# Attention issued in another order over four pairs at once, with the scores on four banks and two banks shared by the rest

## The chip, the cores and the metric

One core of a Trainium2 chip runs the whole program. The metric is the device time of one execution in microseconds (us). The engines are TensorE (PE; its weight loads are listed apart as PEld), VectorE (DVE), ScalarE (ACT), GpSimd (POOL) and SyncE (SP), each with an instruction queue of its own that runs in order and is tied to the others by semaphores only.

## The reference, cut to what matters

The program is four layers one behind the other on `x` of shape (8, 512, 128): attention with relative positions, a mixture of 8 experts, a layer trained at test time, a mixture of 16 experts, each followed by `_layernorm(x + layer(x))`. The change touches the first layer alone:

```python
B, S, D = hidden_states.shape                       # 8, 512, 128; N_HEADS 16, D_KV 64
q = (hidden_states @ Wq).reshape(B, S, N_HEADS, D_KV)      # k and v alike
bias = compute_bias(rel_bias_table, S, S)
scores = jnp.einsum('bqhd,bkhd->bhqk', q, k) * (1.0 / math.sqrt(D_KV)) + bias
attn = jax.nn.softmax(scores, axis=-1)
ctx = jnp.einsum('bhqk,bkhd->bqhd', attn, v).reshape(B, S, N_HEADS * D_KV)
return ctx @ Wo
```

## The kernel before, in words

`kernel` runs `prepare`, `attention`, `ffn_0`, `ttt_layer` and `ffn_1` as phases with a barrier between them. `attention` (L201) works on pairs of heads: 16 heads are 8 pairs, and 8 batches make 64 pairs, one step each, with two more steps to drain. Numbers that need more than fp32r are kept as a high and a low half: ScalarE copies a PSUM bank to fp32r (the high half), VectorE subtracts that from the bank (the low half), and only then is the bank free. A product of two such numbers is three matmuls (`PASSES`).

For one pair the work is:
- TensorE projects q (L386) and k (L387) with `project`, three matmuls of 512 columns each, and one block of values (`make_values`, L308: two token tiles, four heads, six matmuls of 256 columns).
- `scores` (L316), four times, one for each tile of 128 queries: three passes, each for both heads, on the upper and the lower 64 rows, into the two banks `score_ps`. VectorE adds the bias, negates and takes the row's smallest (`score`, L505, and the DVE_READ_ACCUMULATOR behind it); ScalarE takes the exponential and its sum (`exps`, L443).
- `turn` (L326), eight times, four for each head: four transposes of probabilities into one of two banks `turn_ps`, copied by ScalarE (L431) and completed by VectorE (`rest_of_turn`, L515). Turn g waits for the low half of turn g-2.
- `context` (L336), twice: eight matmuls of values with turned probabilities into `ctx_ps`; ScalarE copies it (`copy_context`, L437).
- `add_head` (L349), twice: four fp32 products (eight matmul records) with `wo` into `out_ps`; VectorE scales by the inverse sums (`scale_head`, L523), POOL adds to `x` (`add`, L272).

The order of the work is written out by hand, once for each engine, in `step` (TensorE L358, ScalarE L448, VectorE L532, POOL L280). In step s the scores of pair s stand between the turns, context 0 and output 0 of pair s-1 and output 1 of pair s-2; q and k of pair s+1 are projected in its middle. The values of pairs 0 to 5 are made in their own step, those of pairs 6 and 7 both in step 6 of a batch (`value_pairs`, L263). In step 7, POOL having staged a copy of the next batch's rows (`stage`, L269), TensorE turns x (`turn_rows`, L297) into the only `xT`.

The eight PSUM banks are two for scores, two for turns, two (`misc_ps`) for q, k, values and x, one for contexts, one for outputs. A block of scores therefore waits until VectorE has read the block before (L320).

Of the kernel before, what the change touches and what calls it, by code (L numbers as in the profile page):

```python
# [17 lines left out]
P = 128  # L18
# [182 lines left out]
def attention(core, ins, keep):  # L201
# [4 lines left out]

    nc = core.nc
# [7 lines left out]
    GW = GROUP * D_KV  # L215
    with ExitStack() as st:
        two = lambda name, shape, dt=F32: [core.sb(st, f"{name}{i}", shape, dt) for i in range(2)]

        rows = core.sb(st, "rows", [P, QT, D])
        xT = two("xT", [P, SEQ], F32R)  # L220
        q, k = ([two(f"{n}_{i}", [P, SEQ], F32R) for i in range(2)] for n in "qk")
# [4 lines left out]
        negmax, total = two("negmax", [P, QT, 2]), two("total", [P, QT, 2])  # L226
        inv = [core.sb(st, f"inv{i}", [P, QT, 2]) for i in range(4)]
# [6 lines left out]
        names = ("score_done", "scored", "exp_done", "inv_ready", "turn_done", "turned_hi", "turned_lo", "ctx_done", "ctx_ready",  # L234
                 "val_done", "val_hi", "val_lo", "qk_done", "qk_hi", "qk_lo", "staged", "x_turned", "x_hi", "x_lo", "sum_done", "scaled_ready", "added")
        (score_done, scored, exp_done, inv_ready, turn_done, turned_hi, turned_lo, ctx_done, ctx_ready,
         val_done, val_hi, val_lo, qk_done, qk_hi, qk_lo, staged, x_turned, x_hi, x_lo, sum_done, scaled_ready, added) = (core.sem(n) for n in names)
        block = st.enter_context(nc.Block())

        def steps_of(step):  # L240

            for s in range(STEPS + 2):
                step(s, s // PAIRS, s % PAIRS, s >= STEPS - PAIRS)

        bias_in, wo_in = [core.sem(f"bias_in{i}") for i in range(HEADS // 2)], core.sem("wo_in")
# [11 lines left out]
        is_step = lambda s: 0 <= s < STEPS  # L257
        after = lambda s, n: s >= n
        head = lambda a: slice(a * D_KV, (a + 1) * D_KV)
        tile_of = lambda i: slice(i * P, (i + 1) * P)  # L260
        wide = lambda w, r: w[:, r * P:(r + 1) * P]

        def value_pairs(r):  # L263

            return ((r, 0),) if r < 6 else ((6, 0), (7, 1)) if r == 6 else ()

        @block.gpsimd
        def _(pool):
            def stage(b):  # L269
                pool.tensor_copy(rows[:, :, :], x[:, b * QT:(b + 1) * QT, :]).then_inc(staged, 1)  # L270

            def add(back, b, r, a):  # L272

                pool.wait_ge(scaled_ready, 2 * back + a + 1)
                if after(back, 1) or a:
                    pool.wait_ge(added, 2 * back + a)
                mine = x[:, b * QT:(b + 1) * QT, :]
                pool.tensor_tensor(mine, mine, scaled[a][:, :, :], ALU.add).then_inc(added, 1)  # L278

            def step(s, b, r, last):  # L280
                back, earlier = s - 1, s - 2
                if after(s, 2) and is_step(earlier):
                    add(earlier, b if r >= 2 else b - 1, (r - 2) % PAIRS, 1)
                if after(s, 1) and is_step(back):
                    add(back, b if r >= 1 else b - 1, (r - 1) % PAIRS, 0)
                if r == 3 and not last and is_step(s):
                    pool.wait_ge(x_turned, b + 1)
                    stage(b + 1)

            pool.wait_ge(x_in, 16)  # L290
            stage(0)
            steps_of(step)
            pool.wait_ge(added, HEADS * BATCH)

        @block.tensor
        def _(pe):
            def turn_rows(b):  # L297
                pe.wait_ge(staged, b + 1)
                for j in range(QT):
                    mm = pe.transpose(misc_ps[0][:, tile_of(j)], rows[:, j, :], ident[:, :])  # L300
                mm.then_inc(x_turned, 1)

            def project(to, w, r):
                for n, (u, v) in enumerate(PASSES):
                    mm = pe.matmul(to[:, :], wide(w[u], r), xT[v][:, :], start=(n == 0), stop=(n == 2))
                mm.then_inc(qk_done, 1)

            def make_values(b, n, m):  # L308
                group, first = n // 2, n % 2 * 2
                for t in range(2):  # L310
                    for i, (u, v) in enumerate(PASSES):
                        mm = pe.matmul(misc_ps[m][:, t * GW:(t + 1) * GW], xT[u][:, tile_of(first + t)], wv[v][:, group * GW:(group + 1) * GW],
                                       start=(i == 0), stop=(i == 2))
                mm.then_inc(val_done, 1)

            def scores(s, p, i):  # L316
                if i == 0:
                    pe.wait_ge(qk_lo, 2 * s + 2)
                if after(s, 1) or i >= 1:
                    pe.wait_ge(scored, 8 * s + 2 * i)  # L320
                for n, (u, v) in enumerate(PASSES):
                    for a in range(2):
                        mm = pe.matmul(score_ps[a][:, :], q[p][u][head(a), tile_of(i)], k[p][v][head(a), :], start=(n == 0), stop=(n == 2))  # L323
                mm.then_inc(score_done, 1)

            def turn(back, p, g):  # L326
                a, c = g // QT, g % QT
                if c == 0:
                    pe.wait_ge(exp_done, 8 * back + 7 + a)
                if after(back, 1) or g >= 2:  # L330
                    pe.wait_ge(turned_lo, 8 * back + g - 1)
                for t in range(QT):
                    mm = pe.transpose(turn_ps[g % 2][:, tile_of(t)], prob[p][a][:, t, tile_of(c)], ident[:, :])  # L333
                mm.then_inc(turn_done, 1)

            def context(back, r, a):  # L336

                if after(back, 1) or a:
                    pe.wait_ge(ctx_ready, 2 * back + a)
                if a == 0 and r % 2 == 0:  # L340
                    pe.wait_ge(val_lo, (back - r) + r + 2)
                for c in range(QT):
                    pe.wait_ge(turned_lo, 8 * back + QT * a + c + 1)
                    for n in range(2):
                        mm = pe.matmul(ctx_ps[:, :], val[r // 2 % 2][:, c, r % 2 * 2 + a, :], probT[n][:, c, :],  # L345
                                       start=(c == 0 and n == 0), stop=(c == QT - 1 and n == 1))
                mm.then_inc(ctx_done, 1)

            def add_head(back, b, r, a):  # L349

                pe.wait_ge(ctx_ready, 2 * back + a + 1)
                if after(back, 1) or a:
                    pe.wait_ge(scaled_ready, 2 * back + a)
                for t in range(QT):
                    mm = pe.matmul(out_ps[:, tile_of(t)], ctxT[a][:, tile_of(t)], wo[:, 2 * r + a, :], start=True, stop=True)  # L355
                mm.then_inc(sum_done, 1)

            def step(s, b, r, last):  # L358
                p, back, earlier = r % 2, s - 1, s - 2
                now, turns, sums = is_step(s), after(s, 1) and is_step(back), after(s, 2) and is_step(earlier)  # L360
                br = (r - 1) % PAIRS
                if now:
                    scores(s, p, 0)
                if turns:
                    turn(back, 1 - p, 0)
                    turn(back, 1 - p, 1)
                if now:
                    for n, m in value_pairs(r):
                        make_values(b, n, m)
                    if r == PAIRS - 1 and not last:  # L370
                        turn_rows(b + 1)
                if sums:
                    add_head(earlier, b if r >= 2 else b - 1, (r - 2) % PAIRS, 1)
                if now:
                    scores(s, p, 1)
                if turns:
                    turn(back, 1 - p, 2)
                    turn(back, 1 - p, 3)
                if now and not (last and r == PAIRS - 1):
                    if r == PAIRS - 1:  # L380
                        pe.wait_ge(x_lo, b + 2)
                    elif r == PAIRS - 2:
                        pe.wait_ge(val_lo, PAIRS * b + PAIRS)
                    else:
                        pe.wait_ge(val_lo, PAIRS * b + r + 1)
                    project(misc_ps[1], wq, (r + 1) % PAIRS)  # L386
                    project(misc_ps[0], wk, (r + 1) % PAIRS)  # L387
                if now:
                    scores(s, p, 2)
# [2147 lines left out]
```

## Time and profile before

| | before |
|---|---|
| median of 3 runs | 2408.22 us (2405.91 to 2409.17) |
| the profiled execution | 2398.8 us, span 2397.1 us |
| TensorE busy | 1935.5 us, 81% |
| VectorE busy | 1660.8 us, 69% |
| ScalarE busy | 1198.1 us, 50% |
| POOL busy | 587.8 us, 25% |

The span is the time from the first to the last instruction. Busy time is the union of an engine's instructions. Durations of matmuls overlap, because they are pipelined, so what a matmul holds of the engine is read from the distance to the next start.

### The profile page before, as it was taken

Reading aid. Unit: us, or ns where it says so; the run is one execution under the profiler, and the core shown is the slowest. Engines: PE = TensorE matmul, PEld = TensorE weight load, DVE = VectorE, ACT = ScalarE, POOL = GpSimd, SP = SyncE. Lnnn points to the kernel's source line nnn. Section 1 sums busy time; section 2 is a strip of 40 time slices with the busy share of each in tenths; the row PEclk is TensorE's granted clock in tenths of the full one; section 3 lists DMA queues with packets and bytes.
Section 4 is the critical chain, followed back from the end, with each engine's and each line's share of the span. In section 5 each row is a group of like instructions: output and inputs, shape, how many; then the busy total and the mean of one; then the engine's idle time right before and its main releaser. Section 6 shows DMA issues by size and latency. Waiting matters only on the chain. (4 is left out here: it accounts for less than half of the span.)

```text
span 2397.1 us, 35530 instructions
## 1 busy us (share of the span) xinstructions
PE 1935.5 (81%) x11500; PEld 1484.7 (62%) x11500; DVE 1660.8 (69%) x4000; ACT 1198.1 (50%) x2714; POOL 587.8 (25%) x629
## 2 busy tenths in 40 slices
PE   6999999999999999994789142999989998932771
PEld 4777777777777777773667132777767776711761
DVE  5888888888888888875465677677567755557433
ACT  5777777777777777772033232233223322240432
POOL 0111111111111111110345615443133411000372
PEclk9999999999999999995699566999999999965896
DMA  6000000000000000003044100000000000022243
GB/s 205 1 1 1 1 1 1 1 1 1 1 1 1 1 1 1 1 1 99 27 111 115 49 20 0 1 0 0 1 1 0 0 0 3 1 65 71 74 96 84
DMA packets 60472, 62.37 MB, mean 26 GB/s; under 512 B 6560, under 2 KB 50032, under 8 KB 60064
## 3 DMA queue, kind: packets, MB, share of 16 engines
q1 hardware_dynamic: 49936, 43.79, 5.9%
q0 software_dynamic: 10384, 16.66, 3.5%
q8 instruction: 82, 1.34, 0.2%
q14 instruction: 70, 0.57, 0.1%
HBM read 41.36 MB, written 18.81 MB: 25 GB/s over the span
## 5 line engine op out<-in xcount | busy, mean ns | idle before, releaser
L517 DVE TENSOR_TENSOR probT<-turn_ps,probT 128x512 fp32r<-128x512 f32 x512 | 346.5, 687 | 81.3 <-ACT probT L435 72.1
L445 ACT ACTIVATE prob<-prob,negmax 128x512 f32<-128x512 f32 x512 | 371.2, 725 | 60.8 <-DVE negmax L512 56.9
L278 POOL TENSOR_TENSOR x<-x,scaled 128x512 f32<-128x512 f32 x128 | 165.1, 1290 | 897.2 <-DVE scaled L529 897.2
L435 ACT CAST probT<-turn_ps 128x512 fp32r<-128x512 f32 x512 | 297.2, 581 | 127.7 <-PE turn_ps L333 127.7
L512 DVE CUSTOM_DVE_ANT_0 prob<-score_ps,bias 128x512 f32<-128x512 f32 x512 | 332.4, 686 | 1.4 <-issue 1.4
L333 PE MATMUL turn_ps<-ident,prob 128*128 128x128 f32 x2048 | 290.4, 279 | 39.1 <-DVE probT L517 34.5
L333 PEld LDWEIGHTS turn_ps<-ident,prob 128*128 128x128 f32 x2048 | 223.0, 140 | 137.4 <-DVE probT L517 101.8
L345 PE MATMUL ctx_ps<-probT,val 128*128 128x512 f32 x1024 | 270.1, 405 | 0.0
L323 PE MATMUL score_ps<-k,q 64*128 64x512 f32 x1536 | 247.5, 427 | 5.7 <-DVE negmax L512 4.3
L345 PEld LDWEIGHTS ctx_ps<-probT,val 128*128 128x128 f32 x1024 | 177.8, 188 | 61.8 <-issue 23.0
L323 PEld LDWEIGHTS score_ps<-k,q 64*128 64x128 f32 x1536 | 124.6, 185 | 82.4 <-issue 35.0
L1358 POOL TENSOR_TENSOR w<-c,vc 128x512 f32<-128x512 f32 x64 | 82.9, 1295 | 218.2 <-DVE c L1470 218.2
L355 PE MATMUL out_ps<-wo,ctxT 128*128 128x128 f32 x1024 | 135.4, 275 | 0.7 <-ACT ctxT L441 0.7
L1430 ACT CAST dpT_hi<-pred_ps 128x128 fp32r<-128x128 f32 x64 | 17.1, 267 | 232.6 <-PE pred_ps L1377 232.6
L355 PEld LDWEIGHTS out_ps<-wo,ctxT 128*128 128x128 f32 x1024 | 124.8, 192 | 1.2 <-ACT ctxT L441 1.1
L441 ACT COPY ctxT<-ctx_ps 128x512 f32<-128x512 f32 x128 | 75.7, 592 | 54.8 <-PE ctx_ps L345 54.8
L445 ACT ACTIVATION_READ_ACCUMULATOR prob<-prob,negmax 128x1 f32 x512 | 96.9, 189 | 0.0
L529 DVE TENSOR_TENSOR scaled<-out_ps,inv 128x512 f32<-128x512 f32 x128 | 87.4, 683 | 2.7 <-PE out_ps L355 2.7
L1463 DVE TENSOR_TENSOR s<-u_ps,sg 128x512 f32<-128x512 f32 x64 | 44.3, 692 | 55.6 <-ACT sg L1435 55.6
L939 ACT COPY xgT<-x_ps 128x128 f32<-128x128 f32 x80 | 21.3, 266 | 109.0 <-PE x_ps L887 96.7
L1398 PEld LDWEIGHTS dwp_ps<-dp,h 128*128 128x128 f32 x512 | 67.0, 191 | 5.9
L150 PE MATMUL tt<-ident,x 128*128 128x128 f32 x32 | 6.5, 396 | 79.0 <-PEq L1778 79.0
(489 smaller groups left out, 4095.5 us busy)
## 6 DMA issues: line engine op xcount, KB each, us to landing
ew<-L_ffn_fc_weight SPq DMA_DIRECT2D x32, 256.0 KB
bias<-bias_line SPq DMA_DIRECT2D x16, 448.0 KB, 9.5
mid_rows<-row SPq DMA_DIRECT2D x40, 128.0 KB
last_rows<-row SPq DMA_DIRECT2D x40, 64.0 KB
rows_dram<-rows SPq DMA_DIRECT2D x1, 2304.0 KB, 18.6
acc_dram<-zero POOLq DMA_DIRECT2D x1, 2112.0 KB, 16.9
acc<-acc_dram SPq DMA_DIRECT2D x4, 528.0 KB
x_rows<-x SPq DMA_DIRECT2D x4, 512.0 KB, 6.1
```

Source lines behind the costliest of these rows:

```text
L278: pool.tensor_tensor(mine, mine, scaled[a][:, :, :], ALU.add).then_inc(added, 1)
L323: mm = pe.matmul(score_ps[a][:, :], q[p][u][head(a), tile_of(i)], k[p][v][head(a), :], start=(n == 0), stop=(n == 2))
L333: mm = pe.transpose(turn_ps[g % 2][:, tile_of(t)], prob[p][a][:, t, tile_of(c)], ident[:, :])
L345: mm = pe.matmul(ctx_ps[:, :], val[r // 2 % 2][:, c, r % 2 * 2 + a, :], probT[n][:, c, :], start=(c == 0 and n == 0), stop=(c == QT - 1 an ...
L355: mm = pe.matmul(out_ps[:, tile_of(t)], ctxT[a][:, tile_of(t)], wo[:, 2 * r + a, :], start=True, stop=True)
L435: act.copy(probT[0][:, g % QT, :], turn_ps[g % 2][:, :]).then_inc(turned_hi, 1)
L441: act.copy(ctxT[a][:, :], ctx_ps[:, :]).then_inc(ctx_ready, 1)
L445: act.activation(prob[p][a][:, i, :], prob[p][a][:, i, :], ACT.Exp, bias=negmax[p][:, i, a:a + 1], scale=-1.0, accum_out=total[p][:, i, a: ...
L512: dve.tensor_tensor_reduce(prob[p][a][:, i, :], score_ps[a][:, :], bias[:, h, first:first + SEQ][:, ::-1], -1.0, 3.0e38, ALU.add, ALU.min, ...
L517: dve.tensor_tensor(probT[1][:, g % QT, :], turn_ps[g % 2][:, :], probT[0][:, g % QT, :].bitcast(F32), ALU.subtract).then_inc(turned_lo, 1)
L529: dve.tensor_tensor(scaled[a][:, :, :], out_ps[:, :].rearrange("p (t d) -> p t d", t=QT), inv[r % 4][:, :, a:a + 1].to_broadcast([P, QT, D ...
L1358: pool.tensor_tensor(w[r][:, :], c1[p][:, :], vc[p][:, :], ALU.mult).then_inc(w_ready, 1)
```

## The change

Four pairs are in work at once in `attention`; the arithmetic and the number of instructions stay, but for POOL's copy of the rows and the second wait on exponentials. Scores get four banks, two blocks of two; `work[0]` holds queries, values and context 0, `work[1]` keys, context 1, both outputs and the turned rows. `xT` and the sums get more buffers, x is turned in pair 5 of a batch straight from `x`, and the exponentials count on one semaphore per head. Each engine has one flat list per step. `is_pair(p)` is `0 <= p < 64`, `turns_x(s)` is true in pair 5 of all batches but the last; copies and subtractions are those of before on the new banks.

```diff
-        xT = two("xT", [P, SEQ], F32R)
...
+        xT, q, k = ([two(f"{n}_{i}", [P, SEQ], F32R) for i in range(2)] for n in ("xT", "q", "k"))
...
-        score_ps, turn_ps = [bank("score_ps0"), bank("score_ps1")], [bank("turn_ps0"), bank("turn_ps1")]
-        misc_ps = [bank("misc_ps0"), bank("misc_ps1")]
-        ctx_ps, out_ps = bank("ctx_ps"), bank("out_ps")
...
+        score_ps = [[bank(f"score_ps{i}_{a}") for a in range(2)] for i in range(2)]
+        turn_ps, work = [bank("turn_ps0"), bank("turn_ps1")], [bank("work_ps0"), bank("work_ps1")]
...
         @block.tensor
...
+            def turn_next_rows(s):
+                if turns_x(s):
+                    pe.wait_ge(scaled_ready, 2 * (s - 2) + 2)
+                    turn_rows(batch_of(s) + 1)
...
+            def queries(p):
...
+                    if p % PAIRS == 0:
+                        pe.wait_ge(x_lo, batch_of(p) + 1)
+                    if p >= 1:
+                        pe.wait_ge(val_lo, p)
+                    project(work[0], wq, p)
+            def keys(p):
...
+                    if turns_x(p - 1):
+                        pe.wait_ge(x_lo, batch_of(p) + 2)
+                    elif p >= 3:
+                        pe.wait_ge(scaled_ready, 2 * (p - 3) + 2)
+                    elif p >= 1:
+                        pe.wait_ge(qk_lo, 2 * p)
+                    project(work[1], wk, p)
+            def values(p):
...
+                    if p >= 2:
+                        pe.wait_ge(ctx_ready, 2 * (p - 2) + 1)
...
+            def scores(p, i):
...
+                    if i == 0:
+                        pe.wait_ge(qk_lo, 2 * p + 2)
+                    if p >= 1 or i >= 2:
+                        pe.wait_ge(scored, 8 * p + 2 * i - 2)
+                    for n, (u, v) in enumerate(PASSES):
+                        for a in range(2):
+                            mm = pe.matmul(score_ps[i % 2][a][:, :], q[p % 2][u][head(a), tile_of(i)], k[p % 2][v][head(a), :],
+                                           start=(n == 0), stop=(n == 2))
...
+            def context(p, a):
...
+                    if a == 1:
+                        pe.wait_ge(scaled_ready, 2 * p + 1)
+                    elif p + 2 < STEPS:
+                        pe.wait_ge(qk_lo, 2 * (p + 2) + 1)
...
+            def add_head(p, a):
...
+                    pe.wait_ge(ctx_ready, 2 * p + a + 1)
+                    if a == 0:
+                        if p + 2 < STEPS:
+                            pe.wait_ge(qk_lo, 2 * (p + 2) + 2)
...
+            def step(s):
+                turn(s - 1, 1)
+                add_head(s - 2, 1)
+                queries(s + 1)
+                turn(s - 1, 2)
+                turn(s - 1, 3)
+                turn_next_rows(s)
+                scores(s, 2)
+                scores(s, 3)
+                keys(s + 1)
+                context(s - 1, 0)
+                turn(s - 1, 4)
+                turn(s - 1, 5)
+                scores(s + 1, 0)
+                scores(s + 1, 1)
+                add_head(s - 1, 0)
+                turn(s - 1, 6)
+                turn(s - 1, 7)
+                values(s + 1)
+                context(s - 1, 1)
+                turn(s, 0)
...
         @block.scalar
...
+            def step(s):
+                exps(s, 0, 0)
+                copy_values(s)
+                exps(s - 1, 3, 1)
+                copy_context(s - 2, 1)
+                turn(s - 1, 0)
+                turn(s - 1, 1)
+                exps(s, 0, 1)
+                exps(s, 1, 0)
+                copy_qk(s + 1, 0)
+                copy_next_rows(s)
+                turn(s - 1, 2)
+                turn(s - 1, 3)
+                exps(s, 1, 1)
+                copy_qk(s + 1, 1)
+                copy_context(s - 1, 0)
+                turn(s - 1, 4)
+                exps(s, 2, 0)
+                turn(s - 1, 5)
+                exps(s, 2, 1)
+                exps(s, 3, 0)
+                turn(s - 1, 6)
+                turn(s - 1, 7)
...
         @block.vector
...
+            def step(s):
+                score(s, 0, 1)
+                rest_of_values(s)
+                invert(s - 1)
+                score(s, 1, 0)
+                rest_of_turn(s - 1, 0)
+                rest_of_turn(s - 1, 1)
+                scale_head(s - 2, 1)
+                score(s, 1, 1)
+                rest_of_qk(s + 1, 0)
+                rest_of_next_rows(s)
+                score(s, 2, 0)
+                rest_of_turn(s - 1, 2)
+                rest_of_turn(s - 1, 3)
+                rest_of_qk(s + 1, 1)
+                score(s, 2, 1)
+                score(s, 3, 0)
+                score(s, 3, 1)
+                rest_of_turn(s - 1, 4)
+                rest_of_turn(s - 1, 5)
+                score(s + 1, 0, 0)
+                scale_head(s - 1, 0)
+                rest_of_turn(s - 1, 6)
+                rest_of_turn(s - 1, 7)
```

## Rows read from the trace of the kernel before

**Rows 1.** Stretch, us; busy PE, PEld, DVE, ACT, POOL; PEclk, DMA share, GB/s.

```profile
16.00:1082.60 1066.60, 1014.48 (x6432) 757.79 (x6432) 864.35 (x2184) 815.16 (x1864) 169.37 (x136) 1.00 0.03 9
412.00:543.40 131.40, 126.42 (x805) 94.58 (x804) 107.99 (x273) 101.86 (x233) 21.21 (x18) 1.00 0.00 1
1082.60:2397.10 1314.50, 917.39 (x5064) 726.50 (x5064) 792.99 (x1813) 377.76 (x844) 417.53 (x487) 0.83 0.14 37
```

**Rows 2.** Waits, one batch (412.0 to 543.4 us): total, times, longest.

```profile
PE turn_ps L333 <- DVE probT L517: 4.3, 8, 0.5
```

**Rows 3.** Timeline of TensorE through one pair: start, us, operation.

```profile
444.77 0.98 PE L323 MATMUL score_ps<-k,q 64*128 64x512 f32 x6
445.68 1.09 PE L333 MATMUL turn_ps<-ident,prob 128*128 128x128 f32 x8
446.53 0.36 PE L312 MATMUL misc_ps<-wv_hi,xT 128*128 128x256 f32 x1
...
447.33 1.05 PE L355 MATMUL out_ps<-wo,ctxT 128*128 128x128 f32 x8
448.31 0.97 PE L323 MATMUL score_ps<-k,q 64*128 64x512 f32 x6
449.22 1.09 PE L333 MATMUL turn_ps<-ident,prob 128*128 128x128 f32 x8
450.16 0.73 PE L305 MATMUL misc_ps<-xT,wq_hi 128*128 128x512 f32 x2
450.73 0.39 PE L305 MATMUL misc_ps<-xT,wq_lo 128*128 128x512 f32 x1
450.96 0.62 PE L305 MATMUL misc_ps<-xT,wk_hi 128*128 128x512 f32 x2
451.43 0.40 PE L305 MATMUL misc_ps<-xT,wk_lo 128*128 128x512 f32 x1
451.75 0.97 PE L323 MATMUL score_ps<-k,q 64*128 64x512 f32 x6
452.65 2.13 PE L345 MATMUL ctx_ps<-probT,val 128*128 128x512 f32 x8
454.63 1.03 PE L333 MATMUL turn_ps<-ident,prob 128*128 128x128 f32 x8
455.59 0.96 PE L323 MATMUL score_ps<-k,q 64*128 64x512 f32 x6
456.63 0.66 PE L333 MATMUL turn_ps<-ident,prob 128*128 128x128 f32 x4
457.82 0.66 PE L333 MATMUL turn_ps<-ident,prob 128*128 128x128 f32 x4 [0.53 <-DVE probT L517]
458.31 1.06 PE L355 MATMUL out_ps<-wo,ctxT 128*128 128x128 f32 x8
459.12 2.09 PE L345 MATMUL ctx_ps<-probT,val 128*128 128x512 f32 x8
461.14 0.96 PE L323 MATMUL score_ps<-k,q 64*128 64x512 f32 x6
```

**Rows 4.** Timeline of ScalarE in the same pair.

```profile
455.26 0.59 ACT L435 CAST probT<-turn_ps 128x512 fp32r<-128x512 f32 x1 [0.55 <-PE turn_ps L333]
455.75 0.73 ACT L445 ACTIVATE prob<-prob,negmax 128x512 f32<-128x512 f32 x1
...
456.46 0.57 ACT L435 CAST probT<-turn_ps 128x512 fp32r<-128x512 f32 x1
```

**Rows 5.** Timeline of VectorE in the same pair.

```profile
445.94 0.69 DVE L512 CUSTOM_DVE_ANT_0 prob<-score_ps,bias 128x512 f32<-128x512 f32 x1
...
446.55 0.69 DVE L512 CUSTOM_DVE_ANT_0 prob<-score_ps,bias 128x512 f32<-128x512 f32 x1
...
455.88 0.69 DVE L517 TENSOR_TENSOR probT<-turn_ps,probT 128x512 fp32r<-128x512 f32 x1 [0.20 <-ACT probT L435]
```

**Rows 6.** Timeline of POOL at the start of attention.

```profile
15.79 0.61 POOL L270 COPY rows<-x 128x512 f32<-128x512 f32 x1 [14.26 <-POOLq L79]
```

More of the change, by code:

```diff
@@ L225, in attention @@
         ctxT = two("ctxT", [P, SEQ])
-        negmax, total = two("negmax", [P, QT, 2]), two("total", [P, QT, 2])
-        inv = [core.sb(st, f"inv{i}", [P, QT, 2]) for i in range(4)]
+        negmax = two("negmax", [P, QT, 2])
+        total, inv = ([core.sb(st, f"{n}{i}", [P, QT, 2]) for i in range(4)] for n in ("total", "inv"))
         scaled = two("scaled", [P, QT, D])
@@ L255, in _ @@
                     sp.dma_start(wo[half, :, :], ins["L0_attn_Wo"].rearrange("(h p) d -> p h d", p=D_KV)).then_inc(wo_in, 16)
[L257 to L265, printed above, removed]
         @block.gpsimd
         def _(pool):
[L269 to L288, printed above, removed]
-            pool.wait_ge(x_in, 16)
-            stage(0)
-            steps_of(step)
+            pool.wait_ge(x_in, 16)
+            for p in range(STEPS):
+                mine = x[:, batch_of(p) * QT:(batch_of(p) + 1) * QT, :]
+                for a in range(2):
+                    pool.wait_ge(scaled_ready, 2 * p + a + 1)
+                    if p or a:
+                        pool.wait_ge(added, 2 * p + a)
+                    pool.tensor_tensor(mine, mine, scaled[a][:, :, :], ALU.add).then_inc(added, 1)
             pool.wait_ge(added, HEADS * BATCH)
@@ L304, in project @@
+            def project(to, w, p):
                 for n, (u, v) in enumerate(PASSES):
-                    mm = pe.matmul(to[:, :], wide(w[u], r), xT[v][:, :], start=(n == 0), stop=(n == 2))
+                    mm = pe.matmul(to[:, :], wide(w[u], p), xT[batch_of(p) % 2][v][:, :], start=(n == 0), stop=(n == 2))
                 mm.then_inc(qk_done, 1)
[L308 to L383, printed above, removed]
-                    else:
[L385 to L389, printed above, removed]
-                if turns:
-                    context(back, br, 0)
-                    turn(back, 1 - p, 4)
-                    turn(back, 1 - p, 5)
-                if now:
-                    scores(s, p, 3)
-                if turns:
-                    turn(back, 1 - p, 6)
-                    turn(back, 1 - p, 7)
-                    if s == 1:
-                        pe.wait_ge(wo_in, 32)
-                    add_head(back, b if r >= 1 else b - 1, br, 0)
-                    context(back, br, 1)
@@ new lines, in values @@
+            def values(p):
+                if is_pair(p):
+                    if p >= 2:
+                        pe.wait_ge(ctx_ready, 2 * (p - 2) + 1)
+                    else:
+                        pe.wait_ge(qk_lo, 2 * p + 1)
+                    group, first, xs = p % PAIRS // 2, p % 2 * 2, xT[batch_of(p) % 2]
+                    for t in range(2):
+                        for i, (u, v) in enumerate(PASSES):
+                            mm = pe.matmul(work[0][:, t * GW:(t + 1) * GW], xs[u][:, tile_of(first + t)], wv[v][:, group * GW:(group + 1) * GW],
+                                           start=(i == 0), stop=(i == 2))
+                    mm.then_inc(val_done, 1)
@@ new lines, in turn @@
+            def turn(p, g):
+                if is_pair(p):
+                    a, c = g // QT, g % QT
+                    if c == 0:
+                        pe.wait_ge(exp_done[a], QT * (p + 1))
+                    if p >= 1 or g >= 2:
+                        pe.wait_ge(turned_lo, 8 * p + g - 1)
+                    for t in range(QT):
+                        mm = pe.transpose(turn_ps[g % 2][:, tile_of(t)], prob[p % 2][a][:, t, tile_of(c)], ident[:, :])
+                    mm.then_inc(turn_done, 1)
@@ new lines, in context @@
+            def context(p, a):
+                if is_pair(p):
+                    if a == 1:
+                        pe.wait_ge(scaled_ready, 2 * p + 1)
+                    elif p + 2 < STEPS:
+                        pe.wait_ge(qk_lo, 2 * (p + 2) + 1)
+                    else:
+                        pe.wait_ge(ctx_ready, 2 * (p - 1) + 1)
+                    if a == 0 and p % 2 == 0:
+                        pe.wait_ge(val_lo, p + 2)
+                    for c in range(QT):
+                        pe.wait_ge(turned_lo, 8 * p + QT * a + c + 1)
+                        for n in range(2):
+                            mm = pe.matmul(work[a][:, :], val[p // 2 % 2][:, c, p % 2 * 2 + a, :], probT[n][:, c, :],
+                                           start=(c == 0 and n == 0), stop=(c == QT - 1 and n == 1))
+                    mm.then_inc(ctx_done, 1)
@@ new lines, in add_head @@
+            def add_head(p, a):
+                if is_pair(p):
+                    pe.wait_ge(ctx_ready, 2 * p + a + 1)
+                    if a == 0:
+                        if p + 2 < STEPS:
+                            pe.wait_ge(qk_lo, 2 * (p + 2) + 2)
+                        else:
+                            pe.wait_ge(scaled_ready, 2 * p)
+                    if p == 0 and a == 0:
+                        pe.wait_ge(wo_in, 32)
+                    for t in range(QT):
+                        mm = pe.matmul(work[1][:, tile_of(t)], ctxT[a][:, tile_of(t)], wo[:, 2 * (p % PAIRS) + a, :], start=True, stop=True)
+                    mm.then_inc(sum_done, 1)
@@ new lines, in copy_values, with turn @@
+            def copy_values(p):
+                if is_pair(p):
+                    act.wait_ge(val_done, p + 1)
+                    if p >= 4 and p % 2 == 0:
+                        act.wait_ge(ctx_done, 2 * (p - 3) + 2)
+                    first = p % 2 * 2
+                    act.copy(val[p // 2 % 2][:, first:first + 2, :, 0:D_KV],
+                             work[0][:, :].rearrange("p (t h d) -> p t h d", t=2, h=GROUP)).then_inc(val_hi, 1)
+            def turn(p, g):
+                if is_pair(p):
+                    act.wait_ge(turn_done, 8 * p + g + 1)
+                    if g % QT == 0 and (g or p >= 1):
+                        act.wait_ge(ctx_done, 2 * p + g // QT)
+                    act.copy(probT[0][:, g % QT, :], turn_ps[g % 2][:, :]).then_inc(turned_hi, 1)
@@ L482, in _ @@
             copy_rows(0)
-            copy_qk(0, 0, 0)
-            copy_qk(0, 0, 1)
-            steps_of(step)
+            for s in range(-1, STEPS + 2):
+                step(s)
         @block.vector
@@ L570, in _ @@
             rest_of_rows(0)
-            rest_of_qk(0, 0, 0)
-            rest_of_qk(0, 0, 1)
-            steps_of(step)
+            for s in range(-1, STEPS + 2):
+                step(s)
 class Norms:
```

239 lines of the change are left out of this document (91 added, 148 removed).

## The prediction

> **What bounds the kernel now.** I read the busy time of each engine by stretch first. Attention is the stretch from 16.0 to 1082.6 us, 1066.6 of the 2397.1 us span, and the only one that the diff touches. TensorE is busy for 1014.5 us of it, VectorE for 864.4, ScalarE for 815.2, all at a granted clock of 1.00 (the 2.4 GHz level) [rows 1]. One batch of eight pairs takes 131.4 us, 16.42 us a pair; a plain pair takes 461.14 - 444.77 = 16.37 us [rows 1, 3]. In a pair VectorE is busy 108.0/8 = 13.5 us and ScalarE 101.9/8 = 12.7 us, so TensorE sets the pace: its matmuls lie idle for only 4.3 us per batch, all of it before the turning of probabilities, waiting for VectorE's low half of an earlier turn [rows 2].
>
> Then the timeline of TensorE through one pair, read by the distance from one start to the next, since the durations overlap [rows 3]. What a reader is to see there:
> - A full 512-column matmul holds the engine 0.23 us (450.73 to 450.96). Six projections are 1.39, a context of eight is 1.86, and 1.98 where it follows scores (452.65 to 454.63).
> - A turn of four transposes is 0.44 (eight from 449.22 to 450.16 take 0.94, restart included); an output of eight small matmuls 0.89 (447.33 to 448.31 is 0.98 with the passage to scores); the six 256-column matmuls of the values 0.71 (446.53 to 447.33 with their first load).
> - A block of scores has six matmuls that run two at a time on the upper and lower 64 rows, so three slots, 3 x 0.23 = 0.69. It really takes 0.91 from its first start to the next block's (444.77 to 445.68; 0.90 at 451.75). Ahead of it the preceding block is 0.10 too long (451.43 would be followed at +0.23; the four slots from 450.16 to 451.75 are 1.59 for 1.39, of which about 0.10 is the restart of the first), and the work behind it starts 0.05 to 0.12 slow. So each block alone costs about 0.38 beyond its slots, 1.5 us a pair for four.
> - Two stalls: 455.59 to 456.63 is 1.04 for a block that takes 0.91 (0.13), and 456.63 to 457.82 is 1.19 for a turn of 0.44 (0.70 with its slow restart of 0.05 taken off).
>
> The ledger of a pair: eight turns 3.49, two contexts 3.72, two outputs 1.79, projections 1.39, values 0.71, scores 4 x (0.69 + 0.38) = 4.28: 15.38 us of work. The rest of 16.37, 0.99, is the 0.83 of stalls, two restarts of 0.05 behind them, and 0.05 that I can't place.
>
> **The change, part by part.**
> (1) Scores on four banks in blocks of two. Each pair now issues scores 2 and 3 together, and 0 and 1 of the next pair together. Block 1 no longer waits until VectorE has emptied block 0, so the engine passes into and out of the 64-row form twice a pair and not four times: 2 x 0.38 saved, less the restarts that stay, 0.75 a pair. No row of before has two blocks side by side, so the bounds are: nothing saved, if the six-slot run is broken at its middle, and 0.75. Inside a block the second and third slot follow at 0.23 [rows 3], and the second block has the same shapes and the same rows of the array; I take 0.75.
> For the reason behind the 0.38 the Trainium skill ("TensorEngine Tiling (Array Packing)", Key Properties) has a rule: changing the tiling mode, not just the tile, drains the engine. The trace agrees with a loss at the edges (0.10 ahead of a block, 0.22 in its 0.91 beyond three slots [rows 3]); that it is absent between blocks of the same mode no run here shows yet. By that rule the sum is the one I take; if each block paid it whatever its neighbour, the time would be that of rival B.
>
> (2) The order. Whether the stalls go, I find by walking one pair of the new order with the lengths above. Zero is the start of turn 1 of pair s-1. TensorE without waits: turn 1 at 0; output (s-2, 1) 0.44; queries 1.33; turns 2 and 3 2.02; scores 2 at 3.00, scores 3 at 3.79; keys 4.57; context 0 5.37; turns 4 and 5 7.23; scores 0 and 1 of s+1 at 8.20 and 8.99; output (s-1, 0) 9.77; turns 6 and 7 10.72; values 11.59; context 1 12.33; turn 0 of pair s 14.19; end 14.62. That is the ledger again with half the passages: 3.49 + 3.72 + 1.79 + 1.39 + 0.71 + 3.5 = 14.6.
> The handovers: from the first transpose of a turn to ScalarE's copy 0.63 (454.63 to 455.26), from there to VectorE 0.62 (455.26 to 455.88), from there back to TensorE 0.75 (455.88 to 456.63); from a block of scores to VectorE 1.17 (444.77 to 445.94). On ScalarE a copy holds 0.49, an exponential with its read 0.71; on VectorE an operation holds 0.61 [rows 3 to 5].
> ScalarE then comes out as: context copy (s-2, 1) at -0.23, turn copies 0.25 and 0.72, two exponentials to 2.63, the query copy, turn copies 3.10 and 3.57, an exponential, the key copy not before 5.57 (it waits for the keys, and the context copy and all turns are queued behind it), context copy 7.43, turn copies 7.90 and 9.10, 11.40 and 11.87, values 13.06. VectorE: low halves of turns 0 and 1 at 0.86 and 1.46, scaling 2.07, score (1, 1) 2.67, queries 3.28, score (2, 0) 4.15, turns 2 and 3 4.77 and 5.38, keys 6.17, scores 6.78, 7.40, 8.01, turns 4 and 5 8.62 and 9.70, score and scaling 10.31 and 10.99, turns 6 and 7 12.0 and 12.6, values 13.82, the reciprocals behind the last exponential 14.46, score (1, 0) 14.58.
> Against TensorE's needs: turn 2 needs the low half of turn 0 at 1.61, 0.4 early; scores 3 wait for score (1, 1), 0.3 early; keys for the scaling (2.82), 1.7 early; context 0's fourth chunk for turn 3 (6.13), 0.6 early; scores (s+1, 1) for score (3, 1) at 8.79, 0.2 early; turn 7 for turn 5's low half (10.45), 0.7 early; context 1 for turn 7's (13.35), 1.0 early; output (s-2, 1) needs the context copy at 0.42 and stands at 0.44: no slack at all. So the 0.99 goes, and what is late next is that output, with 0 to 0.2 us a pair. VectorE's 13.5 and ScalarE's 12.7 busy us still fit into 14.62. I take 0.05 for it.
>
> (3) Two shared banks. Queries, values and context 0 pass through one, keys, both outputs, context 1 and x through the other. The waits that this adds are in the walk (keys behind scaling, values behind the context copy of 8.1, context 1 behind the scaling of 11.7) and none is last.
>
> (4) x. Its four transposes stay (0.44 a batch) but move to pair 5, into the second buffer. They wait for the scaling of 2.82 and start at 2.90; the keys behind them start at 5.01 and need x's low half at about 4.93. Gain and loss both under 0.1 a batch. POOL's copy of x's rows goes; it is hidden in seven batches and costs its 0.61 once, at 15.79, where nothing else runs [rows 6]. The additions to x on POOL are the same two per pair, 21.2 us busy in 131.4.
>
> (5) Total buffers, semaphores for exponentials, the order of SP's loads: the same instructions, nothing queued behind them; 0, with ±1 us for both ends of attention. The first pair's lone steps and the last pair's drain keep their chains, only about the last 3 us of each could shift.
>
> The sum: 16.37 - 0.75 - 0.99 + 0.05 = 14.68 a pair. A batch is 8 x 14.68 + 0.44 for x: 117.9 against 131.4, 13.5 a batch, 108 us for eight, and 0.6 at the start. The profiled execution has 2398.8 us around a span of 2397.1 and goes to 2290; the median of the runs shown is 2408.2, 0.4% above it, and goes to 2299. The rest, 1314.5 us at a mean clock of 0.83 [rows 1], is the same program and starts 109 us earlier; that its clock falls and rises at other moments I allow 5 us.
>
> **The rivals.**
> A. New small stalls. In-order ScalarE waits 0.8 us for the keys and 1.4 for context 0 with turns queued behind; if handovers are some tenths slower than my rows, 0.3 to 0.8 us a pair comes back: 64 x 0.3 to 0.8, 2318 to 2350. For it: output (s-2, 1) has no slack, scores only 0.2. Against: most have 0.4 and more.
> B. The double blocks save nothing: +0.75 x 64 = 48, 2347. For it: no row shows such a run, and a wait stands at its middle. Against: waits that are already met cost nothing in the rows of turns and outputs (458.31, 459.12).
> C. The other side: a shared bank is handed over late. A full loop from the writer over ScalarE and VectorE back to the writer is 2.0 us (454.63 to 456.63 [rows 3 to 5]). A pair has seven such handovers on two banks. If one lies bare per pair, it costs 2.0 and eats the whole gain of 1.69: 16.68 a pair, 64 x 0.31 = 20 slower, 2428. It decides from 1.69 us of bare handover a pair. Against: the smallest distance on either bank is 0.1 (x in one pair of eight), else over 1 us.
> D. The change doesn't do what it says: VectorE's queue becomes the pace at its 13.5 busy us plus waits for ScalarE of about 2 (it waits 8 times in my walk): 15.5 a pair, 0.8 x 64 = 51 more, 2350.
>
> **How the numbers follow.** Forecast (2288 to 2312) 0.58; A 0.2; B 0.08; D 0.07; C 0.05; the rest, no change, 0.02. Two executions of one kernel differ by up to 0.14% here, so a difference under 0.2% (5 us) can't be told from none. Faster holds the forecast, A, B and D: 0.93; same 0.02; slower 0.05. The range for 8 in 10 goes from 2285 (no stall at all, clock luck) to 2340, most of A.
>
> **What would show it.** Starts of turn 0 of successive pairs 14.6 to 14.8 us apart; TensorE's idle before turns gone from 4.3 us a batch to under 0.5; the second of two score blocks 0.23 behind the last slot of the first, and six slots from first start to next block in about 1.6; ScalarE waiting once a pair for context 0 and once for the keys; the clock still 1.00. Wrong would be a pair of over 15.2 us, waits at keys, values or context 1 for a scaling (C), or 0.33 and not 0.23 at the middle of a double block (B).

## The result, and the profile after

| | before | changed |
|---|---|---|
| median | 2407.5 us (4 runs) | 2299.4 us (2297.1 to 2300.7, 4 runs) |
| ratio to before | | 0.9555, 95% interval 0.9543 to 0.9568 |
| profiled execution | 2398.8 us, span 2397.1 | 2297.1 us, span 2295.4 |
| attention's last addition ends | 1082.6 us | 980.9 us |
| one pair of heads | 16.37 us | 14.7 us |

The changed kernel is 4.5% faster. Busy times by stretch come first, with the columns of [rows 1]: attention, one batch, and all that follows.

```profile
16.00:980.90 964.90, 953.93 (x6432) 786.27 (x6431) 860.25 (x2184) 797.77 (x1864) 166.57 (x128) 1.00 0.03 10
400.00:517.90 117.90, 117.90 (x805) 97.79 (x804) 107.21 (x274) 99.61 (x233) 20.79 (x16) 1.00 0.00 1
980.90:2295.40 1314.50, 919.43 (x5064) 725.45 (x5064) 793.47 (x1813) 376.74 (x844) 417.72 (x488) 0.83 0.14 37
```

Against [rows 1]: TensorE is busy in all of the 117.9 us, and the clock is 1.00 as before. The two stretches called a batch were cut at 131.4 and 117.9 us; counted from a pair's first scores to those of the eighth pair behind it, and past the first two pairs, a batch takes 131.3 to 131.5 us before and 117.9 to 118.2 after (117.6 at the end, where no x is turned). Behind attention stand the same 1314.5 us at the same mean clock of 0.83. So in the profiled executions all of the 101.7 us lie in attention.

The waits of that batch (total, times, longest). TensorE's matmuls waited for 4.3 us in [rows 2] and have no row any more. The longest waits left, POOL's aside, are those of ScalarE and VectorE, the engines that do not set the pace:

```profile
ACT ctxT L442 <- PE work_ps L358: 10.0, 8, 1.3
DVE probT L521 <- ACT probT L435: 7.3, 23, 0.4
ACT k L419 <- PE work_ps L286: 5.5, 8, 0.8
...
ACT probT L435 <- PE turn_ps L341: 2.5, 8, 0.3
```

TensorE's timeline through one pair, to be read by the distance from start to start as [rows 3]:

```profile
407.15 1.03 PE L341 MATMUL turn_ps<-ident,prob 128*128 128x128 f32 x8
408.02 1.12 PE L373 MATMUL work_ps<-wo,ctxT 128*128 128x128 f32 x8
408.90 0.70 PE L286 MATMUL work_ps<-xT,wq_hi 128*128 128x512 f32 x2
...
409.67 1.03 PE L341 MATMUL turn_ps<-ident,prob 128*128 128x128 f32 x8
410.64 1.66 PE L329 MATMUL score_ps<-k,q 64*128 64x512 f32 x12
412.23 0.73 PE L286 MATMUL work_ps<-xT,wk_hi 128*128 128x512 f32 x2
...
413.03 1.99 PE L358 MATMUL work_ps<-probT,val 128*128 128x512 f32 x8
414.86 1.03 PE L341 MATMUL turn_ps<-ident,prob 128*128 128x128 f32 x8
415.82 1.69 PE L329 MATMUL score_ps<-k,q 64*128 64x512 f32 x12
417.44 1.16 PE L373 MATMUL work_ps<-wo,ctxT 128*128 128x128 f32 x8
418.44 1.04 PE L341 MATMUL turn_ps<-ident,prob 128*128 128x128 f32 x8
419.23 0.36 PE L317 MATMUL work_ps<-wv_hi,xT 128*128 128x256 f32 x1
...
420.02 2.01 PE L358 MATMUL work_ps<-probT,val 128*128 128x512 f32 x8
421.87 1.04 PE L341 MATMUL turn_ps<-ident,prob 128*128 128x128 f32 x8
422.75 1.12 PE L373 MATMUL work_ps<-wo,ctxT 128*128 128x128 f32 x8
```

From 407.15 to 421.87 is 14.72 us. Zero of the prediction's walk is turn 1, half of the first row and of the last but one (two turns each, so 0.44 behind their starts, at 407.59). The walk put the output at 0.44, the queries at 1.33, turn 2 at 2.02, scores 2 at 3.00; the rows have 0.43, 1.31, 2.08 and 3.05. Twelve score matmuls, 410.64 to 412.23, take 1.59 where two blocks of [rows 3] took 0.91 each; from the last slot of the first block to the first of the second are 0.23, as between any two slots. Keys stand at 4.64 (walk 4.57), context 0 at 5.44 (5.37), scores 0 at 8.23 (8.20), output 0 at 9.85 (9.77), turns 6 and 7 at 10.85 (10.72, the largest miss), values at 11.64 (11.59).

ScalarE's copy of context (s-2, 1) in the next pair, the place that the walk gave no slack:

```profile
422.07 0.59 ACT L442 COPY ctxT<-work_ps 128x512 f32<-128x512 f32 x1
```

It ends at 422.66, and the output that needs it starts at 422.75.

### The profile page after: what moved, and what is told of

Same layout as the page of the kernel before. It is cut to its first block and busy times, and to the rows that moved or that the text cites. A ratio compares the mean times of both kernels' runs of the same rounds, so it can differ in the third digit from the quotient of the medians.

```text
span 2295.4 us, 35504 instructions
## 1 busy us (share of the span) xinstructions
PE 1877.2 (82%) x11500; PEld 1512.4 (66%) x11500; DVE 1657.2 (72%) x4000; ACT 1179.7 (51%) x2714; POOL 585.0 (25%) x621
## 5 line engine op out<-in xcount | busy, mean ns | idle before, releaser
L341 PE MATMUL turn_ps<-ident,prob 128*128 128x128 f32 x2048 | 266.3, 273 | 1.3 <-DVE probT L521 1.1
L358 PE MATMUL work_ps<-probT,val 128*128 128x512 f32 x1024 | 257.2, 393 | 0.1
L341 PEld LDWEIGHTS turn_ps<-ident,prob 128*128 128x128 f32 x2048 | 236.7, 140 | 28.2 <-DVE probT L521 3.4
L329 PE MATMUL score_ps<-k,q 64*128 64x512 f32 x1536 | 215.4, 412 | 3.5 <-DVE negmax L515 2.1
L358 PEld LDWEIGHTS work_ps<-probT,val 128*128 128x128 f32 x1024 | 187.4, 188 | 39.9 <-DVE probT L521 1.7
L373 PE MATMUL work_ps<-wo,ctxT 128*128 128x128 f32 x1024 | 146.0, 286 | 0.7 <-ACT ctxT L442 0.7
L373 PEld LDWEIGHTS work_ps<-wo,ctxT 128*128 128x128 f32 x1024 | 123.9, 191 | 26.1 <-issue 22.4
L1423 ACT CAST dpT_hi<-pred_ps 128x128 fp32r<-128x128 f32 x64 | 17.1, 266 | 234.4 <-PE pred_ps L1370 234.4
L442 ACT COPY ctxT<-work_ps 128x512 f32<-128x512 f32 x128 | 75.1, 587 | 84.5 <-PE work_ps L358 83.5
L536 DVE TENSOR_TENSOR scaled<-work_ps,inv 128x512 f32<-128x512 f32 x128 | 87.9, 686 | 2.7 <-PE work_ps L373 2.7
L1399 PE MATMUL pred_ps<-proj,hT 128*128 128x128 f32 x512 | 68.7, 278 | 1.4 <-ACT hT L1437 1.4
```

The source lines that it names most:

```text
L329: mm = pe.matmul(score_ps[i % 2][a][:, :], q[p % 2][u][head(a), tile_of(i)], k[p % 2][v][head(a), :], start=(n == 0), stop=(n == 2))
L341: mm = pe.transpose(turn_ps[g % 2][:, tile_of(t)], prob[p % 2][a][:, t, tile_of(c)], ident[:, :])
L358: mm = pe.matmul(work[a][:, :], val[p // 2 % 2][:, c, p % 2 * 2 + a, :], probT[n][:, c, :], start=(c == 0 and n == 0), stop=(c == QT - 1 a ...
L373: mm = pe.matmul(work[1][:, tile_of(t)], ctxT[a][:, tile_of(t)], wo[:, 2 * (p % PAIRS) + a, :], start=True, stop=True)
L442: act.copy(ctxT[a][:, :], work[a][:, :]).then_inc(ctx_ready, 1)
L536: dve.tensor_tensor(scaled[a][:, :, :], work[1][:, :].rearrange("p (t d) -> p t d", t=QT), inv[p % 4][:, :, a:a + 1].to_broadcast([P, QT, ...
```

## The experiments

**Double blocks taken apart**, both, and one of the two:

```diff
                 scores(s, 2)
-                scores(s, 3)
                 keys(s + 1)
+                scores(s, 3)
...
                 scores(s + 1, 0)
-                scores(s + 1, 1)
                 add_head(s - 1, 0)
+                scores(s + 1, 1)
```

> The changed kernel with both double blocks of scores taken apart: the keys stand between blocks 2 and 3, output 0 between blocks 0 and 1; banks and all other orders as in the change. Theory (a passage into and out of the 64-row form costs about 0.38 us each time, and the double blocks save two of the four): +0.75 us a pair, 64 x 0.75 = 48 us more than the changed kernel's 2299, so 2347; TensorE idle for nothing. Rival (only the new order counts, the passages cost nothing or are hidden): 2299 to 2303.

> Only blocks 2 and 3 taken apart by the keys, blocks 0 and 1 stay together. Theory: one passage more, 0.40 us a pair (exit 0.10, restart of a 512-column matmul 0.11, entry 0.10, slow first slot 0.10), 26 us, so 2325. Rival: nothing, 2299.

Measured: 2350.2 us with both apart (ratio to before 0.978, 0.976 to 0.980), 2330.1 in one run with blocks 2 and 3 apart. The pair is 15.51 and 15.13 us against 14.69: 0.82 for two passages more, 0.44 for one. TensorE's timeline with both apart:

```profile
399.31 1.04 PE L341 MATMUL turn_ps<-ident,prob 128*128 128x128 f32 x8
400.28 0.99 PE L329 MATMUL score_ps<-k,q 64*128 64x512 f32 x6
401.20 0.73 PE L286 MATMUL work_ps<-xT,wk_hi 128*128 128x512 f32 x2
401.77 0.39 PE L286 MATMUL work_ps<-xT,wk_lo 128*128 128x512 f32 x1
402.09 0.96 PE L329 MATMUL score_ps<-k,q 64*128 64x512 f32 x6
402.99 2.11 PE L358 MATMUL work_ps<-probT,val 128*128 128x512 f32 x8
```

Scores 2 are followed after 0.92, the keys' restart (0.57 for two matmuls, 0.34 + 0.23), entry into scores 3 0.32 behind the last key matmul (401.77), scores 3 again 0.90: the pattern of [rows 3] is back. The theory holds and the rival falls. The passages cost slightly more than I had (0.41 to 0.44 and not 0.38 each). In the pair of a batch that turns x the keys, one block earlier here, also wait 0.5 us for the low half of x; plain pairs have no wait of TensorE.

**The shared bank freed late**:

```diff
                 rest_of_turn(s - 1, 1)
-                scale_head(s - 2, 1)
+                if turns_x(s) or not is_pair(s):
+                    scale_head(s - 2, 1)
                 score(s, 1, 1)
...
                 rest_of_turn(s - 1, 3)
+                if is_pair(s) and not turns_x(s):
+                    scale_head(s - 2, 1)
                 rest_of_qk(s + 1, 1)
```

> The changed kernel with VectorE's scaling of output (s-2, 1) moved behind the low halves of turns 2 and 3, except in the pairs that turn x. It frees the shared bank for the keys at 6.74 us of the pair where the keys stand at 4.57. Theory (rival C of the prediction as a mechanism: one bare handover of a shared bank costs TensorE its whole length): 2.17 us a pair in about 55 pairs, 119 us, so 2418, slower than before the change. Rival (the queues have slack enough to take most of it up by shifting): under 1 us a pair, below 2354.

Measured: 2437.8 us, slower than before (1.0128, 1.0109 to 1.0147), as the theory said in its direction, and 20 us beyond its number. The mean pair of most batches is 17.1 us; but for the one that turns x (15.15, its scaling stands where it was) the pairs are of two kinds, 16.7 and 18.25. TensorE's timeline in one of 18.25, and four windows (columns of [rows 1]):

```profile
432.71 1.66 PE L329 MATMUL score_ps<-k,q 64*128 64x512 f32 x12
436.27 1.10 PE L286 MATMUL work_ps<-xT,wk_hi 128*128 128x512 f32 x2 [1.91 <-DVE scaled L536]
437.17 0.63 PE L286 MATMUL work_ps<-xT,wk_lo 128*128 128x512 f32 x1
437.60 3.04 PE L358 MATMUL work_ps<-probT,val 128*128 128x512 f32 x8
440.48 1.04 PE L341 MATMUL turn_ps<-ident,prob 128*128 128x128 f32 x8
```

```profile
423.19:559.81 136.62, 123.29 (x806) 101.28 (x805) 108.37 (x274) 99.62 (x234) 20.71 (x16) 0.96 0.00 1
436.70:439.70 3.00, 3.00 (x8) 2.30 (x7) 1.24 (x4) 0.59 (x1) 0.87 (x1) 0.50 0.00 0
437.60:440.50 2.90, 2.90 (x10) 2.24 (x9) 2.04 (x7) 0.59 (x1) 0.00 (x0) 0.61 0.00 0
444.10:461.10 17.00, 15.10 (x105) 12.52 (x104) 13.79 (x37) 12.63 (x31) 2.57 (x2) 1.00 0.00 0
```

The keys start at 436.27; they were due 1.6 behind the scores, at 434.30. That is the bare handover, 1.97 us. In the pair of 16.7 nothing else happens (window from 444.1, clock 1.00). In the pair of 18.25 the keys take 1.33 us (436.27 to 437.60) where they take 0.80 in the changed kernel, and the context behind them 2.88 (to 440.48) where it takes 1.83: 1.58 together. The granted clock says why: it is 0.50, the lower level of 1.2 GHz, from 436.7 to 439.7, and 0.61 over the whole context. The stall of 1.9 us once a pair had gone before, and TensorE was busy otherwise. So a bare handover costs its length and, in 21 of the 54 pairs that have it (mostly three of a batch), 1.6 us more through the clock: 54 x 1.97 + 21 x 1.6 = 140 us, and attention's last addition ends 139.3 us later than in the changed kernel (1120.2 against 980.9). Why one pair falls and the next, with the same stall, does not, no run shows.

The Trainium skill describes such a thing ("TensorE: Matmul & The Clock Gate", A second HAM failure mode: psum-queue depth-cycling): where a kernel cycles through PSUM banks, short idles between groups of matmuls make the clock swing between its two levels, and throughput is lost to the throttling and warming up. This run's trace agrees in the swing, with 0.96 over the batch; the next experiment, with a shorter stall, does not show it.

**The copy without slack, one place later**:

```diff
-                copy_context(s - 2, 1)
                 turn(s - 1, 0)
+                copy_context(s - 2, 1)
                 turn(s - 1, 1)
```

> The changed kernel with ScalarE's copy of context (s-2, 1) one place later, behind the copy of turn 0. Theory (output (s-2, 1) has no slack, so any delay of that copy goes straight into the pair): the copy starts 0.72 instead of -0.23 us, the output 0.93 late, 62 x 0.93 = 58 us, 2357, and no change of the clock, since the stall is under 1 us. Rival (the clock falls here as it does with longer stalls): 2375 or more. Second rival (slack in the queues takes it up): under 2315.

Measured: 2357.1 us in one run; the pair 15.6 us, 0.93 more. TensorE's timeline, turns 0 and 1 and the output behind them:

```profile
401.09 1.03 PE L341 MATMUL turn_ps<-ident,prob 128*128 128x128 f32 x8
402.85 1.16 PE L373 MATMUL work_ps<-wo,ctxT 128*128 128x128 f32 x8 [0.72 <-ACT ctxT L442]
...
416.71 1.04 PE L341 MATMUL turn_ps<-ident,prob 128*128 128x128 f32 x8
418.48 1.16 PE L373 MATMUL work_ps<-wo,ctxT 128*128 128x128 f32 x8 [0.73 <-ACT ctxT L442]
```

From the turns' start to the output are 1.76 us; in the changed kernel they were 0.88 (421.87 to 422.75). The whole delay comes through, and the clock stays at 1.00 in attention, so both rivals fall.

**VectorE loaded with one more operation** (result unused):

```diff
                 scale_head(s - 2, 1)
+                if is_pair(s):
+                    dve.tensor_tensor(spare[1][:, :], bias[:, 0, 0:SEQ], bias[:, 1, 0:SEQ], ALU.add)
                 score(s, 1, 1)
```

> The changed kernel with one more 128x512 sum of two SBUF tensors on VectorE in each pair, ahead of score (1, 1); its result is not used. Theory (VectorE has about 1.6 us of waits in a pair, and the place has 0.33 us of slack towards scores 3): of its 0.61 us only 0.28 shows, 64 x 0.28 = 18 us, 2317. Rival D of the prediction (VectorE's queue is all but the pace): the full 0.61, 39 us, 2338.

Measured: 2315.9 us in one run, 14.98 us a pair: 0.29 of 0.61 show. The place's slack takes up the rest, so VectorE's queue is not the pace; rival D of the prediction is out.

**Scores on all 128 rows** (both heads' rows summed into each bank, so not the reference's scores):

```diff
-q[p % 2][u][head(a), tile_of(i)], k[p % 2][v][head(a), :]
+q[p % 2][u][:, tile_of(i)], k[p % 2][v][:, :]
```

> The changed kernel with its score matmuls on all 128 rows and not on 64 (both heads' rows are summed into each bank, so the scores are other numbers; the count of matmuls, banks and waits stay). No block is of the 64-row form any more, but the two of a pass run one behind the other: 24 slots of 0.23 = 5.52 us a pair for 12 slots and two passages, 3.5. Theory (the 0.38 us of a passage are the price of changing the form): 14.69 + 2.0 = 16.7 us a pair, 64 x 2.0 = 129 us, 2428. Rival (they come from starting any block of scores, whatever its form): 0.75 more, 17.45 us a pair, 2476.

Measured: 2422.0 us in one run, 16.58 us a pair. TensorE's timeline, turns, a double block, keys:

```profile
427.88 1.03 PE L341 MATMUL turn_ps<-ident,prob 128*128 128x128 f32 x8
428.68 2.99 PE L329 MATMUL score_ps<-k,q 128*128 128x512 f32 x12
431.50 0.61 PE L286 MATMUL work_ps<-xT,wk_hi 128*128 128x512 f32 x2
```

Entry and exit cost next to nothing: eight transposes are followed after 0.80, where scores of the 64-row form follow them after 0.97 (409.67 to 410.64), and 12 matmuls take 2.82, the first 0.31 and the others 0.23 each; the first key matmul behind them takes 0.23 and not 0.34. The rival's 17.45 is far off. So the 0.4 us belong to changing the form, not to starting scores. Why a change of form costs them, no run shows.

**The old order with one edit on ScalarE** (kernel before):

```diff
-                for a in range(2):
-                    if now:
-                        exps(s, p, 2, a)
+                if now:
+                    exps(s, p, 2, 0)
+                for a in range(2):
                     if turns:
                         turn(back, 4 + a)
+                if now:
+                    exps(s, p, 2, 1)
```

> The kernel before the change with one edit on ScalarE: the copies of turns 4 and 5 both ahead of the exponential (2, 1), not around it. Theory (the 0.70 us stall of before comes from turn 5's copy standing 0.72 us behind an exponential, so that TensorE's turn 7 waits for its low half): the low half of turn 5 starts right behind that of turn 4, 0.58 us earlier, turn 7 follows, 0.58 x 63 = 36 us less than before's 2407.5: 2371. Rival (the stall only moves, to the delayed exponential or to the context): 2400 to 2410.

Measured: 2373.4 us, ratio 0.9876 (0.9857 to 0.9895); the pair 15.82 and not 16.34 us. TensorE's timeline at the old stall:

```profile
412.03 0.96 PE L323 MATMUL score_ps<-k,q 64*128 64x512 f32 x6
413.07 1.25 PE L333 MATMUL turn_ps<-ident,prob 128*128 128x128 f32 x8
414.16 1.06 PE L355 MATMUL out_ps<-wo,ctxT 128*128 128x128 f32 x8
414.97 2.18 PE L345 MATMUL ctx_ps<-probT,val 128*128 128x512 f32 x8
```

Scores 3 still take 1.04, but turns 6 and 7 follow each other in 1.09 where [rows 3] has 456.63 to 458.31, 1.68. So 0.53 us a pair of the change's gain were to be had by one edit in the old order, and the rival (the stall only moves) falls.

**Another drain**, twice. The last pair turns its probabilities through the free score banks (`turn_bank` takes the two turn banks, then the four of the scores); in the second form output (63, 0) has a free bank too and context (63, 0) stands ahead of turns 4 and 5:

```diff
+        last_banks = turn_ps + score_ps[0] + score_ps[1] + turn_ps
+        turn_bank = lambda p, g: last_banks[g] if p == STEPS - 1 else turn_ps[g % 2]
...
+        out_bank = lambda p, a: score_ps[0][0] if (p, a) == (STEPS - 1, 0) else work[1]
```

> The changed kernel with another drain: the last pair turns its probabilities through the four score banks, which are free by then, so turns 2 to 5 wait for no low half, and the scaling of output (62, 1) stands behind the low halves of turns 2 and 3. Theory (the drain is set by the round trip of two turn banks): the time from the last turn 0 to the last addition falls from 14.6 to about 13 us, 1.5 us in all, 2298. Rival (the drain is set by the copies and low halves in their order, whatever the banks): no change within 0.5 us of attention's end.

> The drain once more: as in the wide tail, but context (63, 0) stands ahead of turns 4 and 5, and output (63, 0) has a bank of its own (a free score bank), so that context (63, 1) waits for no scaling. Theory (in the wide tail the gain of the free banks was eaten by turns 4 and 5 ahead of the context and by the shared bank, 1.25 us of wait for the scaling): from the last turn 0 to the last addition 12.4 us and not 14.6, 2.2 us less than the changed kernel. Rival (the drain is bound by copies and low halves): 14 us or more. In the whole time 2 us can't be told from noise; the profile decides.

> The changed kernel again, on the chip of the other drain, for a comparison: 2297 to 2301, attention's last addition ends near 980.9 us, 14.6 us behind the last turn 0.

The first form missed: 2304.8 us (2296.4 to 2306.3), ratio 0.9566 (0.9548 to 0.9583), and its drain took 14.62 us like the changed kernel's, as its rival had it. Turns 2 to 5 came early, but the context had to wait behind turns 4 and 5, and context 1 for the scaling of output 0:

```profile
973.45 2.11 PE L367 MATMUL work_ps<-probT,val 128*128 128x512 f32 x8 [1.25 <-DVE scaled L557]
```

The second form, and the changed kernel on the same chip, each by the last start of turn 0 (first row) and POOL's last addition:

```profile
967.99 1.03 PE L351 MATMUL turn_ps<-ident,prob 128*128 128x128 f32 x8
...
979.78 1.26 POOL L272 TENSOR_TENSOR x<-x,scaled 128x512 f32<-128x512 f32 x1 [1.57 <-DVE scaled L558]
```

```profile
966.68 1.03 PE L341 MATMUL turn_ps<-ident,prob 128*128 128x128 f32 x8
...
980.04 1.26 POOL L269 TENSOR_TENSOR x<-x,scaled 128x512 f32<-128x512 f32 x1 [3.50 <-DVE scaled L536]
```

981.04 - 967.99 = 13.05 against 981.30 - 966.68 = 14.62: 1.57 us, not 2.2, but enough to put the rival (14 or more) out: the banks, with the order on them, set at least this much of the drain. In the whole time they are 2285.1 (2283.3 to 2286.1) and 2285.8 (2283.6 to 2290.8), ratios 0.9565 (0.9552 to 0.9578) and 0.9575 (0.9561 to 0.9590) to a kernel before that ran in 2388.1 there: a version no slower than the changed kernel, and not shown to be faster.

## Why the prediction was right

The forecast was 2299 us, the median 2299.4. The mechanism and the size of a pair were right; the terms were off by up to 0.1 us a pair in opposite directions, and the ends of attention by more.

(1) The double blocks. Taken as 0.75 us a pair out of bounds of 0 and 0.75; undone, they cost 0.82 (15.51 against 14.69). The ledger of a passage (0.38) was 0.03 short. Rival B is out: the wait at the middle costs nothing, its step is 0.23 and not 0.33, and twelve matmuls run in 1.59 us.

(2) The order and its stalls. The prediction had 14.68 a pair; plain pairs are 14.67 to 14.79, the batch 117.9 to 118.2 for 117.9. With 0.82 for the double blocks, 16.35 - 14.69 - 0.82 leaves 0.84 for the order where 0.94 were forecast: TensorE has no stall, the 0.05 for the late output was not needed, but the walk's 14.62 came out as 14.7. Of the 0.84 one stall of the old order, 0.53, is shown by itself; the rest was not isolated. The place named as late next was right, and the late copy shows how sharp it is: 0.93 us of delay give 0.93. The slack of 0.3 ahead of scores 3 is right too: an operation of 0.61 there showed 0.29. Rival A did not come.

(3) The shared banks. Rival C was a real danger. Its handover was sized right (1.97 for 2.0), and its price was too low: laid bare in 54 pairs and not 64 it gives 2438 and not 2428, since the clock falls with it. The order keeps every handover covered.

(4) x is where it was put: a batch (but the last) holds one pair of 15.13 to 15.22 us, 0.44 more, nothing beside it. The small margin of the keys there (5.01 against 4.93) was real: one block earlier they waited 0.5 us.

(5) The ends are the term that was off. I let all 64 pairs save their 1.7 us, and allowed ±1 for fill and drain, so 109 in all; the profiled executions differ by 101.7. The first score block moved from 23.3 to 22.6 us as said (0.7). But the scores of the last pair now start half a pair ahead of their place, and the drain behind them is longer. In both kernels, the last pair's scores 0 and POOL's last addition, before:

```profile
1052.58 0.96 PE L323 MATMUL score_ps<-k,q 64*128 64x512 f32 x6
...
1081.30 1.26 POOL L278 TENSOR_TENSOR x<-x,scaled 128x512 f32<-128x512 f32 x1 [2.08 <-DVE scaled L529]
```

and changed:

```profile
947.13 1.68 PE L329 MATMUL score_ps<-k,q 64*128 64x512 f32 x12
...
979.64 1.26 POOL L269 TENSOR_TENSOR x<-x,scaled 128x512 f32<-128x512 f32 x1 [3.51 <-DVE scaled L536]
```

30.0 us before (1082.56 - 1052.58), 33.8 after (980.90 - 947.13): 3.8 us given back, and 63 distances between pairs, not 64, save 1.7. The first batch saved 12.9 where 13.5 were forecast, 0.6 less, and the 55 distances behind it 91.8 for 92.8, 1.0 less. The start gave 0.1 more than forecast. That is the whole of the 7 us.

That the medians differ by 108.1 all the same was not in the working: the profiled execution of before lies 0.4% under its median and that of the changed kernel 0.1%. The profiles of all runs show where executions differ: the part behind attention, the same program in each, took from 1302.8 to 1322.1 us, while the plain pairs of the two kernels repeat within 0.15. That it took 1314.5 in both profiles above is chance, and so a difference of medians can lie several us off what attention saves. The prediction's 0.14% between executions was too small: its profiled execution already lay 0.4% off. What varies behind attention stays open. Another chip ran both kernels 14 to 20 us faster with attention ending at 981 us as here; there the medians differ by 102.3 (2388.1 and 2285.8), by what attention saves. So the agreement to a microsecond is luck: the term for attention was 7 us too large, and the executions made up for it. That to 0.3% is not.

## What to carry to other kernels

Where one engine is busy 95% of a stretch, count what holds it from start to start, not its busy time: passages between row forms and restarts are in there, and grouping blocks of one form removes them. In a loop of in-order queues, a walk of one period with measured handover times tells which wait has slack; here it was right to 0.13 us at every place of TensorE, and its tightest place was where a delay of one copy cost its full length. Then count the periods between the ends, not the loop's iterations, and walk the drain as well.

## What the runs showed of the hardware that was not expected

A stall of 1.9 us per pair (about one in 17 us) with TensorE busy otherwise was enough for the clock to fall to its lower level in 21 of 54 pairs: for about 3.4 us from just behind the stall a 512-column matmul took 0.43 us for 0.23, 1.6 us on top. The delay of 0.9 us per pair of the late context copy left it at 1.00. Sizes between these two were not tried.

An output whose copy by ScalarE ended 0.09 us before its first matmul still ran without a stall (422.66 and 422.75).
